# Clustering and averaging merged into one pass, and eight-row transfers in the last pass of a gated convolution kernel

## What is computed

```
# layer 0
x0   = conv 3x3, stride 2, 2 channels -> 1 (512 -> 256 channels, 64x64)      # "downsampled"
xs   = rows of x0[0] scaled to 0..1                                            # 256 rows of 4096
labels = kmeans(xs, 8 clusters, 10 rounds) ; one more assignment
v5   = mean of x0[b] over the channels of each cluster                          # 8 x 8 x 4096
mu, var = mixture of 2 Gaussians fitted to v5[b], 10 rounds
gate = sigmoid(combination of mu with w_conv)[labels]
x1   = bilinear_x2(repeat((gate + 1) * x0, 2) * w_up) + x
# layer 1
xP   = x1 projected on 64 cosine products P (128x128 -> 64)
Q, K, V from xP; norms lamdq, lamdk per position; A = P^T (P / lamdk)
out  = gamma * (V-part of (A, K, Q) / lamdv + bias) + x1
```

## Time and profile before

| | |
|---|---|
| median of 3 runs | 3865.55 us |
| the profiled execution: its own time | 3863.4 us |
| its span | 3861.8 us |
| first pass, to the first issue of clustering | 0 to 1367.6 us |
| clustering | 1367.6 to 1515.8 us |
| averaging | 1515.8 to 1811.9 us |
| mixture | 1811.9 to 2038.6 us |
| last pass, prologue | 2038.6 to 2129.4 us |
| last pass, 8 images | 2129.4 to 3861.8 us |

### The profile page before, as it was taken

How to read it: one execution, slowest core, us unless ns; L and a number is a source line. 1 busy time by engine, 2 the same in 40 slices (tenths; PEclk the granted TensorE clock), 3 DMA queues, 4 the chain that set the end, 5 groups by cost and what they waited for, 6 DMA issues and landing times. The chain is left out here.

```text
span 3861.8 us, 68816 instructions
## 1 busy us (share of the span) xinstructions
PE 3209.1 (83%) x23738; PEld 2390.1 (62%) x23738; DVE 3018.2 (78%) x3491; ACT 1871.3 (48%) x4272; POOL 645.3 (17%) x325
## 2 busy tenths in 40 slices
PE   7999999999999745998556887888889887888877
PEld 3454554545455345776334787877778787877777
DVE  5999999999999933113443897979889797979877
ACT  4555555555555310222221555555655556555654
POOL 0000000000000000000000333333333333333333
PEclk9999999999999865998666999999999999999999
DMA  6646556556556212221002899999999999999998
GB/s 275 254 201 259 243 206 264 231 219 264 220 231 265 116 73 98 102 116 44 0 0 78 289 345 322 348 327 346 346 340 343 326 343 337 343 325 347 353 349 305
DMA packets 348925, 945.54 MB, mean 245 GB/s; under 512 B 25937, under 2 KB 58833, under 8 KB 329490
## 3 DMA queue, kind: packets, MB, share of 16 engines
q1 hardware_dynamic: 339346, 907.41, 63.3%
q0 software_dynamic: 9216, 33.56, 2.1%
HBM read 638.90 MB, written 301.99 MB: 244 GB/s over the span
## 5 line engine op out<-in xcount | busy, mean ns | idle before, releaser
L189 DVE SCALAR_TENSOR_TENSOR first_acc<-first_x,first_wd,first_acc 128x1024 f32<-128x1024 f32 (+1 forms) x1088 | 1297.8, 1275 | 57.4 <-ACT first_acc L214 46.0
L1172 PE MATMUL second_o<-second_right,second_left 128*128 128x128 f32 x8192 | 1106.9, 286 | 186.5 <-POOL second_left L964 121.1
L1172 PEld LDWEIGHTS second_o<-second_right,second_left 128*128 128x128 f32 x8192 | 1023.0, 200 | 239.7 <-issue 211.2
L964 POOL TENSOR_TENSOR second_left<-second_mid_copy,second_coef_rep 64x1024 f32<-64x1024 f32 x256 | 610.6, 2385 | 1881.9 <-ACT second_mid_copy L1278 1876.4
L1417 DVE SCALAR_TENSOR_TENSOR second_x<-second_o,second_shift,second_x 128x512 f32<-128x512 f32 x1024 | 734.1, 738 | 233.5 <-PE second_o L1172 231.1
L218 ACT ACTIVATE first_xT<-first_tp 128x512 f32<-128x512 f32 x1024 | 608.3, 597 | 533.6 <-PE first_tp L244 533.0
L244 PE MATMUL first_tp<-all_const,first_x 128*128 128x128 f32 x4096 | 679.4, 291 | 79.8 <-issue 41.5
L244 PEld LDWEIGHTS first_tp<-all_const,first_x 128*128 128x128 f32 x4096 | 441.3, 143 | 461.1 <-issue 444.4
L256 PE MATMUL first_freq<-first_xT,all_p 128*64 128x256 f32 x4096 | 667.4, 407 | 17.7 <-ACT first_xT L218 8.1
L1257 ACT ACTIVATE second_mid<-second_dd,all_inter 128x128 f32<-128x128 f32 x1024 | 327.1, 390 | 386.0 <-DVE second_mid L1399 374.7
L256 PEld LDWEIGHTS first_freq<-first_xT,all_p 128*64 128x64 f32 x4096 | 210.6, 136 | 193.9 <-issue 178.8
(11 more groups left out here) (215 smaller groups left out, 2327.3 us busy)
## 6 DMA issues: line engine op xcount, KB each, us to landing
second_x<-in_x SPq DMA_DIRECT2D x512, 512.0 KB, 7.5
out<-second_x SPq DMA_DIRECT2D x512, 512.0 KB, 5.7
first_x<-in_x SPq DMA_DIRECT2D x48, 4224.0 KB, 25.3
first_x<-in_x SPq DMA_DIRECT2D x16, 4096.0 KB
second_dd<-downsampled SPq DMA_DIRECT2D x112, 384.0 KB, 6.4
downsampled<-first_acc POOLq DMA_DIRECT2D x64, 512.0 KB, 11.6
average_xd<-downsampled SPq DMA_DIRECT2D x16, 2048.0 KB, 8.4
second_dd<-downsampled SPq DMA_DIRECT2D x16, 320.0 KB, 6.2
```

Source lines behind the costliest of these rows:

```text
L189: nc.vector.scalar_tensor_tensor(out=acc[c][:, :, left:], in0=tap_window(xt[c], (s, dh, dw), OUT1), scalar=wd[:, t, k:k + 1], in1=acc[c][: ...
L964: return eng.tensor_tensor(left[a][rows, odd:HALF:2, :, :].rearrange("p n (t s) g -> p n t s g", t=T), turned[rows, :, :, :].unsqueeze(3). ...
L1172: last = nc.tensor.matmul(ob[n][:, r, :], left[a][:, r, n, :], right[a][:, r, :], start=True, stop=True)
```

## The change

**Clustering and averaging become `gather_pass`.** One loop over k runs on PE and ACT. For k from 0 to 127 it makes one unit of the cosine rows of x0: 4 transposes, one ACT copy of 512 columns, 2 matmuls of 64 stationary and 256 moving columns in the two column halves (as the first pass does), 16 units for each image. Into it are placed the transposes for clustering (k from 10 to 17 and from 22 to 29), the product `gram` (8 matmuls at each k from 31 to 38), and the 11 rounds (one third of a round at each k from 40 to 72). The cluster means follow from k = 80: 16 matmuls of 32 stationary and 512 moving columns, four column groups side by side, for each image, four of them between units and four behind the loop. The result leaves by eight DMAs of 32 KB for each image from a row buffer into `ft`. The last four images that are averaged are loaded a second time.

**The last pass** loads, adds to and stores x in chunks of eight rows (2 DMAs of 1024 KB each way, 4 buffers instead of 8, three chunks ahead). The downsampled rows come once, four rows for each chunk, into a ring of 16 rows. The weighting of a chunk needs the last row of the chunk before and the first row of the next one, so `weight(m, 0)` waits for chunk m+1 too. The coefficients are replicated image by image in the `stage` work (PE at u = 17, ACT at u = 18) rather than for all images ahead of the loop. The cosine table `p` is freed after the first pass and loaded again (4 MB) in the prologue. There the stage work of image 0 comes first and `weight` behind it.

The core of the diff, in the order PE and SP of `gather_pass`, then the sizes of the last pass, SP's `load_rows` and `step`, ACT's `weight` and PE's `replicate`:

```diff
+                for k in range(ends):
+                    x = x_group(k)
+                    if x:
+                        turn_x(*x)
+                    if GRAM_AT <= k < GRAM_AT + GROUPS:
+                        make_gram(k - GRAM_AT)
+                    if ITER_AT <= k < ITER_AT + 3 * (ITERS + 1):
+                        iterate(k - ITER_AT)
...
+                    if k < units:
+                        turn(k)
+                    if 2 <= k < units + 2:
+                        multiply(k - 2)
+                    b, u = k // UNITS_F - 1, k % UNITS_F
+                    if b >= 0 and u == 5:
+                        join(b)
+                    if k >= EARLY * UNITS_F and k % UNITS_F == 0:
+                        average(k // UNITS_F - EARLY)
+                for n in range(B // 2, B):
+                    average(n)
...
+                for n, b in enumerate(MEAN_ORDER):
+                    sp.wait_ge(mean_taken, n + 1)
+                    for r in range(POS // 512):
...
+                        sp.dma_start(flat[b * 2 * K:(b + 1) * 2 * K, r * 512:(r + 1) * 512],
+                                     rows_sb[n % 2][at:at + 2 * K, :]).then_inc(rows_out[n % 2], 16)
+                    if n < EARLY - 1:
+                        load(RING_OF_MEAN[n + B // 2], MEAN_ORDER[n + B // 2])
...
-XBUF = 8
-AHEAD = XBUF - 2
+XBUF = 4
+AHEAD = XBUF - 1
...
-                    sp.wait_ge(weighted, b * CH2 + m + CHUNK_LEAD - 1)
...
-                    first, last = max(n * DROWS - 1, 0), min(n * DROWS + DROWS + 1, HD)
...
-                    sp.dma_start(dd[slot][:, :, at:at + last - first, :].rearrange("g t h w -> g t (h w)"),
-                                 rows[:, :, first * WD:last * WD]).then_inc(dd_in[slot], 16)
+                    sp.wait_ge(weighted, b * CH2 + m - 2 + CHUNK_LEAD)
+                    rows = xd[b + m // CH2].rearrange("t g n -> g t n")
+                    sp.dma_start(dd[:, :, slot * DROWS:(slot + 1) * DROWS, :].rearrange("g t h w -> g t (h w)"),
+                                 rows[:, :, n * DROWS * WD:(n + 1) * DROWS * WD]).then_inc(dd_in[slot], 16)
...
-                    if u % 2 == 1 and (more or chunk_of(u) < CH2 - 3):
-                        load_rows(b, chunk_of(u) + 3)
-                    store(b, u)
-                    if more or u + AHEAD < UNITS:
-                        load_image(b, u + AHEAD)
+                    m = chunk_of(u)
+                    if u % 2 == 1 and (more or m < CH2 - 3):
+                        load_rows(b, m + 3)
+                    if u % 2 == 1:
+                        store(b, m)
+                    if u % 2 == 1 and (more or m + AHEAD < CH2):
+                        load_image(b, m + AHEAD)
...
+                        if m == 0:
+                            act.wait_ge(dd_in[0], b * (CH2 // DSLOTS) * 16 + 16)
+                        if n + 1 < CH2:
+                            act.wait_ge(dd_in[(m + 1) % DSLOTS],
+                                        (b * (CH2 // DSLOTS) + loads + (n + 1) // DSLOTS + 1) * 16)
...
+                def replicate(q):
+                    pe.wait_ge(coef_picked, q + 1)
+                    pe.wait_ge(lam2_made, q * 4 + 4)
+                    for n in range(TS):
+                        last = nc.tensor.matmul(st[:, 512 + n * P:512 + (n + 1) * P],
+                                                coef_q[:, n:n + 1].broadcast_to([P, P]), k("ident"),
+                                                start=True, stop=True)
```

More of the change, by code:

```diff
@@ L410, in _, with turn_x @@
[L410 to L413 removed]
+                pe.wait_ge(const_in, 16)
+                def turn_x(t, n):
+                    if n == 0:
+                        pe.wait_ge(normal, t + 1)
+                    done = t * GROUPS + n
+                    if done >= 2:
+                        pe.wait_ge(x_copied, done - 1)
+                    for a in range(4):
+                        at = (4 * n + a) * P
+                        last = nc.tensor.transpose(bank_x[n % 2][:, a, :], xx[t][:, at:at + P], ident)
+                    last.then_inc(x_turned, 1)
@@ L414, in _, with make_gram @@
+                def make_gram(g):
+                    t, first = g // (GROUPS // 2), g % (GROUPS // 2) * 8
+                    if g == 0:
+                        pe.wait_ge(x_copied, T * GROUPS)
+                    for n in range(first, first + 8):
+                        last = nc.tensor.matmul(gram_ps[:, t, :], xsT[:, n, t, :],
                                                 xsT[:, n, :, :].rearrange("p t g -> p (t g)"),
                                                 start=n == 0, stop=n == NT - 1)
-                    last.then_inc(gram_made, 1)
@@ new lines, in make_gram, with iterate @@
+                    if first + 8 == NT:
+                        last.then_inc(gram_made, 1)
+                def iterate(step):
+                    i, what = step // 3, step % 3
+                    if what == 0:
+                        if i == 0:
+                            pe.wait_ge(gram_copied, 1)
+                        pe.wait_ge(moved, i + 1)
+                        for t in range(T):
+                            for t2 in range(T):
+                                last = nc.tensor.matmul(dot_ps[:, t * K:(t + 1) * K], gram[:, t2, t * P:(t + 1) * P],
+                                                        wt[:, t2, :], start=t2 == 0, stop=t2 == T - 1)
+                        last.then_inc(dots, 1)
+                    elif what == 1:
+                        pe.wait_ge(prods, i + 1)
+                        for t in range(T):
+                            last = nc.tensor.matmul(c2_ps[:, 0:K], ones, prod[:, t, :], start=t == 0, stop=t == T - 1)
+                        last.then_inc(c2s, 1)
+                    else:
+                        pe.wait_ge(labelled, i + 1)
+                        for t in range(T):
+                            last = nc.tensor.matmul(count_ps[:, 0:K], ones, oh[:, t, :], start=t == 0, stop=t == T - 1)
+                        last.then_inc(counted, 1)
@@ new lines, in multiply @@
+                def multiply(k):
+                    b, u, slot = k // UNITS_F, k % UNITS_F, k % SLOTS
+                    if u == 0 and b >= 2:
+                        pe.wait_ge(freq_read, b - 1)
+                    pe.wait_ge(copied[slot], k // SLOTS + 1)
+                    for n in range(2):
+                        last = nc.tensor.matmul(freq_ps[b % 2][n * UV:(n + 1) * UV, 0:T * P], q_sb[:, 2 * u + n, :],
+                                                dT[slot][:, n, :], start=u == 0, stop=u == UNITS_F - 1)
+                    last.then_inc(multiplied[slot], 1)
@@ L882 @@
 SET_UP = 5
-CHUNK_LEAD = 2
+CHUNK_LEAD = DSLOTS
 TURN_LEAD = 3
@@ L1219, in _, with stage @@
                 act.sem_inc(weighted, CHUNK_LEAD)
-                def stage(q, u):
+                def stage(q, u, first=False):
+                    if u == 18:
+                        act.wait_ge(coef_turned, q + 1)
+                        if not first:
+                            act.wait_ge(coef_in, q)
+                        nc.scalar.activation(coef_next[:, :], st[:, 512:1024], ACT.Copy).then_inc(coef_copied, 1)
                     if u == 2:
@@ L1287, in prologue @@
                 def prologue():
-                    for b in range(B):
-                        act.wait_ge(coef_turned, b + 1)
-                        nc.scalar.activation(coef_all[:, b, :], zt_t[:, :, :].rearrange("p n g -> p (n g)"), ACT.Copy
-                                             ).then_inc(coef_copied, 1)
+                    for u in range(UNITS):
+                        stage(0, u, True)
                     for m in range(2):
@@ L1294, in prologue @@
                             weight(0, m, e)
-                    for u in range(UNITS):
-                        stage(0, u)
                     copy(0, 0)
```

492 lines of the change are left out of this document (235 added, 257 removed).

## The result

The changed kernel took 4126.55 us in the median of 4 runs (4124.80 to 4129.84), the kernel before 3862.46 us on the same chip (4 runs, 3852.54 to 3874.26). The ratio is 1.068 (95% interval 1.066 to 1.070): slower by 264 us, where 4045 us, or +182, had been predicted. The profiled execution has a span of 4125.4 us.

A forecast was written before the change was run, and what follows sets the result against it. The prediction took engines handing work to each other, not the DMA engines, as the bound; 3863.4 - 162 (merged pass) - 20 (last pass's start) + 360 (its loop) + 3 gave 4044, predicted as 4045 us, range 3850 to 4260 us.

The forecast's parts named there:

- Part 3: Loop of the last pass: downsampled rows land after `weight` wants them, costing +45 us an image, +360 us for eight.
- The landing: Last pass's loop: the downsampled rows, 4.46 MB in all with those ahead, land 13.3 us after the store.
- The clock: Last pass's loop: PE drops to the lower clock level after idling, 1.3 us for each even unit.
- the relief at the boundary: Last pass's loop: most of an image's 13.6 us of boundary and stage work falls into waits, -11 us.
- The queue is served in order: Last pass's loop: rows land only behind the 4.2 MB of stores and loads issued earlier in the same queue.
- Part 1: Merged clustering and averaging pass: 283 us instead of 444.3, a gain of 162 us, with bounds 175 and 90.
- The tail: End of the merged pass: copy, small DMA issues, last image's second load, its average and a landing, 28 us.
- Part 2: Start of the last pass: replication and first `weight` no longer ahead of stage work, `p` load hidden, gain 20 us.
- A: Rival, last pass's loop: rows land in time, `weight` does not wait, 3684 us in all; chance 0.12.
- B: Rival, last pass's loop: DMA engines are the pace and the loop gains with fewer bytes, 3634 us; chance 0.02.
- C: Rival, last pass's loop: wait holds the boundary too, clock stays low, +75 us an image, 4285 us; chance 0.07.
- D: Rival, last pass's loop: landing at 11.4 us with the clock kept, 3834 to 3890 us in all; chance 0.09.

## Why the prediction was right, and where its sizes were off

**Part 3 was right in its mechanism.** ACT waits in `weight(m+2, 0)` for the rows of chunk m+3, with the copy for GpSimd and PE behind it; taking the wait away gives the whole loss back. Of the signs that were named, these are there: rows landing 9.7 us after their issue (9 to 10 forecast), a DMA share of 0.71 (0.75), a clock of 0.87 (below 0.90), and 16.7 us for a chunk (268.0 us for an image by 16; 16.4 forecast). What was off:

- The landing, 14.5 us behind the store instead of 13.3. I had summed bytes by bandwidth and one latency. SP first needs 4.5 us to issue two stores and two loads, and the rows 9.9 us on average from there. At a microsecond for each pair these 1.2 us are 72 us of the loop, and the miss there is 48.
- The clock (1.3 us for each pair) and the relief at the boundary (11 us an image). Both were too large. The clock term should show between `weight(m+2, 0)` and the store of chunk m+1. For chunks 3 to 15 of an image this way averages 18.54 us in the profile before and 18.76 us in the changed one: 0.2 us, not 1.3, although PE starts at half speed after a long wait (row at 2369.36). For chunks 0 to 2, where the boundary and the heavier stage pieces lie, it falls from 21.2 to 18.9 us. Since two chains run side by side, that is worth half of three times 2.3 us, some 3.5 us an image by this estimate. In the sum the two terms were 78 us on one side and 88 on the other. That their errors cancel is luck.
- The pattern. Forecast were 110 to 125 waits of 2 to 6 us. There were 85, up to 12.1 us, and 627.6 us in all, not 300 to 500. A store gates `weight` of three chunks on, which gates the store two chunks on, so the even and the odd chunks form two chains that run through each other. The length of a pair varies little (33.5 us in the median); how it splits drifts (12.2 and 23.2 us at one place, 16.1 and 16.1 at another).
- "The queue is served in order" gave nearly the right number from a reason that is too narrow. In a queue of their own the rows landed 14.1 us behind the store on average, against 14.5.

**Part 1 gained 130 us, not 162.** The transposes for clustering cost less: a unit with them is 1.60 us (1395.73 to 1397.33), not 2.05, since ACT keeps up, which is 7 us instead of 14. The rounds cost more. While the granted clock was 1.00 a round took 6.10 us, and 6.2 was forecast. After three of them the clock fell to 0.50, the 1.2 GHz level, and stayed there until the rounds were over. On average a round took 8.8 us (1467.30 to 1555.28), 58 us beyond the units instead of 30. "The small matmuls run at the full clock" is the step that failed, and the rounds two units apart show it: same matmuls, same DVE chains, clock 1.00, and 38 us less than in the same kernel with the rounds close together (322.5), some 7 us of which are the spacing itself. The sum's bound of 16 us for the rounds has no working behind it: its own case of a perfect fit, 3.5 us a round, is 38 us. The tail took 38 us, not 28:

```profile
1646.42 5.54 SPq L392 DMA_DIRECT2D gates_ft<-gather_rows  x8
...
1652.00 1.06 SPq L360 DMA_DIRECT2D gather_d<-downsampled  x2
...
1653.11 27.73 SPq L392 DMA_DIRECT2D gates_ft<-gather_rows  x32
...
1668.43 6.01 PE L613 MATMUL gather_count_ps<-gather_d,gather_placed 128*32 128x512 f32 x32 [10.48 <-issue]
...
1683.38 0.31 SPq L698 DMA_DIRECT2D mix_wc<-in_w_conv  x1
```

The last load waits for the 5.5 us of small issues ahead of it in SP's queue and takes 16 us from there (1652.00 to 1668.43), the last average takes 6.0 us at the low clock, and 9 us of issues and landing follow (1674.44 to 1683.38). 7 us gained, 28 and 10 lost: 31 of the 32.

The Trainium skill's rule on drains (TensorEngine Tiling (Array Packing), Key Properties) had given a gain of 130 us, and the gain is 130 us, but not for that reason. An average between units takes 22.7 us with its 16 units (1574.57 to 1597.29), 4.0 more than the units alone and 3.64 of it matmuls, so 0.4 us are left for the two changes. At that price the 41 places would cost 16 us, an estimate, and not 32. The kernel with the rounds further apart has as many changes and is 38 us faster in this pass.

**Part 2 was right:** 71.0 us where 71 were forecast, and no wait for `p`.

**The rivals.** A, rows in time at 3684 us, is what the kernel with the rows one chunk earlier is, at 3709; the difference is part 1's, whose pass took 322.5 us there and so gained 40 us less than summed, less the 12 us that the loop gained. B falls: with no late rows and 1 MB transfers the loop takes 1720.3 us at a DMA share of 0.88, 12 us less than before the change, and the engines' handoffs pace it as before. C, 600 us more in the loop, and D, 150 us with a landing at 11.4 us, did not come: the loop's 411 us lie nearest the forecast, on C's side of it.

## What to carry to other kernels

When a ring replaces buffers with their own halo, the last row of a step becomes an input of the step before: move its transfer up by one step in the same edit, and count what each issuing queue and the transfer engines still hold at that moment. A wait on an in-order engine costs what stands behind it, so put it in front of the first instruction that reads the data and not at the head of the step. Small latency-bound matmuls can be hidden between dense ones, but space them so that the clock stays up, and read the granted clock of that stretch before believing a sum.

## What the runs showed of the hardware

- PE can be busy all the time at the low clock. From 1485 to 1556 us its rows fill 71.0 of 71.0 us at a granted 0.50, and just before, at 89% busy (1466 to 1485), it had 1.00. At half speed the same work leaves no gaps, and it did not come back up until the 8-column matmuls ended. The Trainium skill (TensorE: Matmul & The Clock Gate, Part 1: The HAM clock gate) has the gate follow how busy the array has been, with activity releasing it; the busy share of these rows does not decide it, and the measurement stands. The fall came after one, two or three rounds in the eight profiles with the rounds close together, and the merged pass took 312.8 to 322.5 us in them.
- A 256 KB transfer in ACT's queue, which held nothing else in the loop, took 9.9 us with 2 MB of loads issued 2.7 us before it on SP's (and 2 MB of stores 1.5 us before those), and 3.9 us when the loads were 9.7 us old. Over the loop it landed 12.6 us behind the first load on average, whenever it was issued.
- Four issues of 1 MB and four of 512 KB took SP the same 4.5 us, addresses and waits included.
